# Selective scan on one core: two of VectorE's instructions in each chunk moved ahead of a product

## The reference

```python
x_dbl = jnp.einsum('kcd,bkdl->bkcl', x_proj_w, xs)
dts, Bv, Cv = jnp.split(x_dbl, [R, R + N], axis=2)          # R = 12, N = 4
dt = jnp.einsum('kdr,bkrl->bkdl', dt_proj_w, dts) + dt_proj_b[None, :, :, None]
dt = jax.nn.softplus(dt)
A = -jnp.exp(A_log)
def step(h, inp):
    dt_t, u_t, B_t, C_t = inp
    dA = jnp.exp(dt_t[..., None] * A)
    h = dA * h + dt_t[..., None] * B_t[:, :, None, :] * u_t[..., None]
    y = jnp.einsum('bkdn,bkn->bkd', h, C_t)
    return (h, y)
```

## Time and profile before

| what | value |
|---|---|
| median of 3 runs | 9437.26 us (9434.93 to 9440.56) |
| the profiled execution | 9426.04 us, its span 9424.2 us |
| PE (TensorE) busy | 8659.1 us (92%), granted clock 0.975 of full in the mean |
| DVE (VectorE) busy | 7371.5 us (78%), 8225 instructions |
| ACT (ScalarE) busy | 6096.1 us (65%) |
| POOL (GpSimd) busy | 3293.4 us (35%) |
| recurrences L1217 | 1536, 1882.7 us busy |
| products L1225 | 768, 937.5 us busy |

### The profile page before, as it was taken

How to read it: one execution, slowest core, us unless ns; L and a number is a source line. 1 busy time by engine, 2 the same in 40 slices (tenths; PEclk the granted TensorE clock), 3 DMA queues, 4 the chain that set the end, 5 groups by cost and what they waited for, 6 DMA issues and landing times. The chain is left out here.

```text
span 9424.2 us, 104196 instructions
## 1 busy us (share of the span) xinstructions
PE 8659.1 (92%) x26436; PEld 4640.1 (49%) x26436; DVE 7371.5 (78%) x8225; ACT 6096.1 (65%) x7436; POOL 3293.4 (35%) x1874
## 2 busy tenths in 40 slices
PE   7899988999889998899988999889998899988999
PEld 3336733367333673336733367333673336633366
DVE  6987769876698766987679876798767987679876
ACT  6765667656675566755667556675566755677555
POOL 2860028600385003850038500385003850038500
PEclk9999999999999999999999999999999999999999
DMA  1320013200132001320013200132001320023200
GB/s 52 116 79 11 11 53 111 80 11 11 55 115 76 11 10 55 116 75 10 12 58 111 75 10 12 60 114 71 10 12 60 116 68 10 12 66 110 68 12 12
DMA packets 286693, 503.21 MB, mean 53 GB/s; under 512 B 142155, under 2 KB 143215, under 8 KB 253431
## 3 DMA queue, kind: packets, MB, share of 16 engines
q1 hardware_dynamic: 286199, 497.81, 17.7%
HBM read 467.99 MB, written 29.47 MB: 53 GB/s over the span
## 5 line engine op out<-in xcount | busy, mean ns | idle before, releaser
L1363 DVE TENSOR_TENSOR pl<-pf,ph 128x1024 fp32r<-128x1024 f32 x1024 | 1254.1, 1225 | 1014.2 <-ACT ph L1003 1008.0
L1217 DVE TENSOR_TENSOR_SCAN h<-ps,h,dbu 128x512 f32<-128x512 f32 x1536 | 1882.7, 1266 | 52.2 <-POOL dbu L1068 29.9
L1068 POOL TENSOR_TENSOR dbu<-bs,du 128x1024 f32<-128x1024 f32 x768 | 1808.5, 2370 | 54.1 <-POOL du L1059 54.1
L1003 ACT ACTIVATE ph<-pf 128x1024 fp32r<-128x1024 f32 x1024 | 1085.7, 1060 | 753.5 <-PE ps L695 753.2
L867 ACT ACTIVATE ps<-dt,negA 128x512 f32<-128x512 f32 x1536 | 1037.9, 687 | 720.4 <-DVE h L1217 720.1
L1023 POOL MEMSET sqb<- 64x512 f32 x16 | 8.3, 519 | 3985.4 <-issue 3980.4
L997 ACT ACTIVATE pf<-ps 128x1024 f32<-128x1024 f32 x1024 | 1051.0, 1026 | 534.9 <-PE ps L682 534.9
L1347 DVE TENSOR_REDUCE mx<-ps 128x1 f32<-128x512 f32 x1792 | 1167.9, 683 | 78.7 <-PE ps L600 60.5
L1225 DVE TENSOR_TENSOR hc<-h,ps 128x1024 f32<-128x1024 f32 x768 | 937.5, 1221 | 113.9 <-PE ps L481 20.0
L481 PE MATMUL ps<-xhl,selr 128*128 128x512 f32 x1536 | 756.2, 577 | 259.8 <-DVE hc L1225 259.5
L1053 POOL TENSOR_TENSOR dt<-dt,ze 128x1024 f32<-128x1024 f32 x256 | 604.5, 2361 | 1044.0 <-ACT dt L860 1043.9
(11 more groups left out here) (200 smaller groups left out, 14514.2 us busy)
## 6 DMA issues: line engine op xcount, KB each, us to landing
bs<-rows SPq DMA_DIRECT2D x256, 1024.0 KB, 5.2
bs<-rows SPq DMA_DIRECT2D x512, 256.0 KB, 6.1
xa<-in_x SPq DMA_DIRECT2D x130, 256.0 KB, 2.9
xb<-in_x SPq DMA_DIRECT2D x130, 128.0 KB, 3.0
out<-fa SPq DMA_DIRECT2D x64, 256.0 KB, 2.1
rdb<-rden SPq DMA_DIRECT2D x56, 192.0 KB, 3.6
out<-fa SPq DMA_DIRECT2D x64, 128.0 KB, 2.4
xhl<-ct SPq DMA_DIRECT2D x256, 8.0 KB
```

The costliest lines, as they stand in the source:

```text
L1003: A(ph[:, mp % 2, :, :], pf[:, mp % 2, :, :], ACT.Copy).then_inc(S["ph_ready"], 1)
L1068: pool.tensor_tensor(dbu[:, q, :, :], bs[par][:, q, :, :], du[:, r:r + 1, :].to_broadcast([P, 2, T]), ALU.mult).then_inc(S["dbu_ready"], 1)
L1217: dve.tensor_tensor_scan(h[:, j, ::step], ps[:, 2 + e, ::step], dbu[:, q, e, ::step], h[:, j, end:end + 1], ALU.mult, ALU.add)\
L1363: TT(pl[:, mp % 2, :, :], pf[:, mp % 2, :, :], ph[:, mp % 2, :, :].bitcast(F32), ALU.subtract)\
```

## The change

Only the order on VectorE changes. `softplus` now stands between the first pair's recurrences and the first product with C. The first recurrence of the third pair stands between the second pair's recurrences and the second product; its second recurrence stands behind that product. `scans` gets a parameter for the half, and repeats its wait on `dbu_ready` in each call. The other engines' streams are the same.

```diff
-                def scans(k, q, s):
+                def scans(k, q, s, halves=(0, 1)):
...
-                    for e in range(2):
+                    for e in halves:
...
-                    for q in range(NP):
-                        s = g * NP + q
-                        scans(now[0], q, s)
-                        times_c(q, s)
-                        if q == 0 and nxt:
-                            if not before:
-                                residue(g + 1)
-                            softplus(1 - par, g + 1)
+                    k, s = now[0], g * NP
+                    scans(k, 0, s)
+                    if nxt:
+                        if not before:
+                            residue(g + 1)
+                        softplus(1 - par, g + 1)
+                    times_c(0, s)
+                    scans(k, 1, s + 1)
+                    scans(k, 2, s + 2, (0,))
+                    times_c(1, s + 1)
+                    scans(k, 2, s + 2, (1,))
+                    times_c(2, s + 2)
```

## The result

The changed kernel takes 9579.35 us in the median of 4 runs (9573.29 to 9580.42), the kernel before 9437.17 us; the ratio is 1.0149 with a 95% interval of 1.0131 to 1.0167. It is slower by 142 us. The prediction was 9554 us, range 9500 to 9610.

A forecast was written before the change was run, and what follows sets the result against it. The prediction took a ring from VectorE through TensorE's queue and ScalarE to bound the changed kernel: 9426 + 87 (10.8 us an image, eight images) + 30 for the clock = 9543, with 11 to the median 9554 us; range 9500 to 9610.

The forecast's parts named there:

- Sum on VectorE: VectorE, each chunk: two of three dependent starts go, 2 x 0.19 = 0.38 us saved.
- The ring: VectorE-TensorE-ScalarE loop: later product delays spread, projection, softplus work, decay, next recurrence; second-half chunks 13.91 against 13.40 us.
- First half: Chunks whose ScalarE also writes xsf: 15.02 against 14.48 us, +4.1 an image; five others 14.07 against 14.38, -1.6.
- VectorE alone would need 14.00, so the ring is last there too: First-half chunks without the xsf write: the ring's 14.07 us, not VectorE's 14.00, sets their length.
- Chunk 0: First chunk of an image: softplus waits for POOL's sum, so the projection starts later, +1.9 us.
- The clock: TensorE's granted clock falls at the projection in one of six second-half chunks, +1.7 us each, +30 us in all.
- block of 2.0 us: TensorE, second half: idle time gathers into one 2.0 us block ahead of the spread in every chunk.
- The end of the image: Chunks 30 and 31, reckoned with 14, 15 and 23: shorter rings or a reset, together about -0.2 us an image.
- the cover of the third pair's first decay: ScalarE: this decay has from 5.95 to 7.03 us for its 0.72 us, so its cost was put at nothing.
- VectorE is the bound: Rival: VectorE's saving comes through, 0.38 x 256 = 97 us, 9340 us; chance 0.07.
- Nothing is won on VectorE: Rival: after a recurrence even an unrelated operation starts 0.12 us late; +43 us, 9597 us; chance 0.10.
- The clock in most chunks: Rival: the clock falls in most of the thirteen second-half chunks, 140 to 177 us, about 9680 us; chance 0.09.

The follow-up runs named there:

- the softplus half alone: Kernel before with only softplus moved ahead of the first product, all six recurrences in their old places; 9567.20 us.
- the projection ahead: The whole change, plus on TensorE the dt projection placed ahead of the spread for pair 1; 9361.51 us.
- the filler: The whole change, plus in the second half TensorE spreads the C rows of pair 0 twice; 9554.73 us.
- another kernel: The change with dt projection first, third pair whole in the last chunk, and the spread of pair 1 done twice in chunk 30; 9339.79 us.

## Why the prediction was right, and where it was off

- **Sum on VectorE.** Two starts a chunk were saved, 0.38 us worked out, 0.42 measured (13.40 to 12.98) once nothing else closed last.
- **The ring.** The step that decided, the spread held by the later product and the projection behind it, is shown from both sides: swapping the two on TensorE gives the gain back, and the softplus half alone carries the loss. 13.91 us worked out, 13.96 measured, 0.51 and 0.56 us of loss a chunk.
- **First half.** In the xsf chunks the mechanism holds and the term was mis-sized: the spread was taken to hold TensorE's queue for its busy time, 0.73 us, where the next work starts after 0.57. The rows of the changed kernel (chunk start 362.97):

```profile
367.72 0.73 PE L481 MATMUL ps<-xhl,selr 128*128 128x512 f32 x2 [0.76 <-DVE hc L1225]
368.29 1.88 PE L468 MATMUL ps<-xd,wdt 128*128 128x512 f32 x4
...
377.67 2.46 DVE L1217 TENSOR_TENSOR_SCAN h<-ps,h,dbu 128x512 f32<-128x512 f32 x2 [0.33 <-ACT ps L867]
```

  With that and the projection's own 1.88 us instead of 1.98 the chunk takes 14.70 us where 15.02 was forecast. In the chunks without the xsf write a step failed: "VectorE alone would need 14.00, so the ring is last there too". The first recurrence that ends such a chunk (start 334.35) waits for no decay:

```profile
334.35 2.46 DVE L1217 TENSOR_TENSOR_SCAN h<-ps,h,dbu 128x512 f32<-128x512 f32 x2 [0.33 <-ACT ps L867]
...
348.27 2.46 DVE L1217 TENSOR_TENSOR_SCAN h<-ps,h,dbu 128x512 f32<-128x512 f32 x2
```

  VectorE is last there, with 13.92 us where 14.07 was forecast; it has the same 13.92 with the projection ahead. Both together are nearly all of the 28 us.
- **Chunk 0.** +1.9 us forecast, +1.7 measured.
- **The clock.** One in six chunks was chosen, +30 us. Measured +42 us: 45 of the 104 chunks are longer than 14.11 us, but mostly by less than the 1.7 us of a whole projection (0.9 on average). There were more such chunks than chosen and each cost less; that the product came near is luck. The block of 2.0 us "in every chunk" is not there in every chunk: 36 of the 104 have 1.8 us or more ahead of the spread, and 32 of these are long; of the other 68, 13 are. From chunk 25 on the block is 0.9 us at most, and behind a long chunk it is often shorter too.
- **The end of the image.** Chunks 30 and 31 were reckoned by VectorE's saving, -0.4 us. The step that failed: the cover of the third pair's first decay, from 5.95 to 7.03, was checked for a chunk in the middle of the stage and not for the last one, where the decay stands behind sums that are late. With it went the first product, which waits for a spread behind the same sums. Measured +3.6 us an image, 29 us; keeping the third pair whole in chunk 31 gives back 21 of them.
- The first half, 28 us too high, and the end of the image, 32 us too low, nearly cancel, which is luck. The 11 us outside the scan stage had no term in the sum.
- Of the rivals, "VectorE is the bound" describes the kernel with the projection ahead, where it has its 0.42 us; in the change it is refuted. "Nothing is won on VectorE" is refuted by softplus, which starts 2.38 us after the recurrences' start, 0.08 us before their end. The clock in most chunks: not reached, 45 of 104. The section that the prediction names for the rival, "The DRAIN you can't avoid" of "VectorE: DVE Perf Modes" in the Trainium skill, also says that a next operation that is not held starts earlier; so the 1.14 us of the earlier trace rows does not contradict it.

## What to carry to other kernels

Before work is reordered on the busiest engine, list what each moved instruction releases and what stands behind the released work in the other engine's queue. Here one product became late by 0.92 us, and a projection that had nothing to do with it paid, since it stood behind the product's follower. VectorE was ahead of the ring by 0.25 us only, and the move made the ring itself 0.8 us longer, so its own saving of 0.4 us a chunk could not show. Look at the wait that ends last, and move the two queues together. Check the last turn of a loop on its own rows.

## What was unexpected of the hardware

The granted clock reacted to idle blocks of 1 to 2 us. With blocks of 1.8 to 2.03 us in a third of the second-half chunks it fell from 1.00 to 0.88 there; behind blocks of 1.13 and 0.78 us in one chunk it fell too (0.52 in the stretch shown). With the filler, blocks of 1.1 us left it up in eight of eight images in chunk 20 and not in chunk 17, and in chunk 30 of another kernel it fell behind a block of 0.97 us. So the length of one block does not foretell it. An operation that does nothing useful made the kernel some 20 us faster. In the first half a spread that is busy for 0.73 us lets the next matmul start after 0.57 us.
